# The expert stage of a graph and mixture-of-experts kernel in 68 pairs of 128-row halves, with the rows as weights of the first product

## The chip, the cores and the metric

The kernel runs on one core of one Trainium2 chip. The metric is the device time of one execution in microseconds; the number for a kernel is the median of its runs. The engines are named as the profile names them: PE is TensorE (PEld its weight loads), DVE is VectorE, ACT is ScalarE, POOL is GpSimd, and SP is SyncE, which issues most of the DMAs. A q behind a name (PEldq, SPq) is an engine's own queue: what waits, issues DMAs or computes register values there.

## The reference, cut to what matters

The input is 128 samples of 128 rows of 384 values, 16384 rows (tokens) in all. First come two graph layers per sample. Then each row goes through one of eight experts, the one that a small router gives the highest probability. Only this second half is touched.

```python
x = x + graph_layers(layernorm(x), adj, ...)          # (128, 128, 384)
# expert half: H = 384, R = 64, E = 8
def ffn(x, enc_w, enc_b, sw_w, sw_b, w1, b1, w2, b2):
    xt = x.reshape(-1, d)
    route_prob = softmax((xt @ enc_w + enc_b) @ sw_w + sw_b, axis=-1)
    route_prob_max, routes = max(route_prob), argmax(route_prob)
    onehot = one_hot(routes, E)
    h = einsum('td,edr->ter', xt, w1) + b1[None]
    h = gelu(h) * onehot[..., None]
    out = einsum('ter,erd->td', h, w2) + onehot @ b2
    return out * route_prob_max[:, None]
x = x + ffn(layernorm(x), ...)                        # layernorm: (x - mean) / sqrt(var + 1e-5)
```

## The kernel before

The program has two stages, each a block of five instruction streams, one for each engine, with semaphores between them; all engines meet at the border of the blocks.

**The graph stage** works on one sample at a time, two units of work a step in a software pipeline, and takes most of the time. Beside the graph layers it computes, for each finished sample, the layernorm's scale and shift and the router's choice, and scatters the rows into a DRAM buffer `buckets`, one region per expert, with an indirect DMA on GpSimd (L1236). A bucket row has 388 words: 384 values, the scale, the shift, the probability and the row's ID. After the last sample VectorE computes in `tile_table` (L1009 on) where each tile starts in `buckets` and which expert it has; eight expert numbers are packed in one word of `expert_words`.

**The expert stage** (L1358 on) cuts each expert's rows into tiles of 256 rows, T = 2 halves of P = 128. TILES is 16384 / 256 + 8 = 72, enough for every way in which the rows may fall on the experts; the last tile of an expert is moved back so that it ends with the expert's rows, and a row that comes twice gets an ID out of bounds (`again`), so that its second store is dropped. Everything is unrolled: `tiles` calls `step(i, i % 8)` on each engine for i from 0 to 76, and a step does several tiles at different points of the pipeline. For tile j:

- SyncE (`load`, L1415) reads the start row from `tile_row` and loads the tile into `tok`, a ring of eight, two neighbouring bucket rows (3104 bytes) to a partition. It does so only in the second block, after all scatters have landed.
- ScalarE and VectorE each normalise one half (L1492, L1541) into `n2_rows`; ScalarE also copies the expert's w1, doubled to 128 columns, into `w1_pick` (L1500), and its bias into `b1_pick` (L1504).
- TensorE turns the six 128 x 128 blocks (L1445, a turn is a product with the identity); ScalarE and VectorE copy them from PSUM to `n2T` (L1510, L1548).
- TensorE multiplies (`hidden`, L1457): weights `w1_pick` (128 columns), moving `n2T` (256 rows of the tile), three parts of the inner length 384. The type is f32, and each such product stands in the trace as two records. The result has the 64 hidden values twice, on 128 partitions, and the tile's rows along the columns.
- ScalarE applies GELU with the bias (L1519); VectorE splits the result into a high part and a low part (L1554, L1558), both on 128 partitions.
- TensorE multiplies each half with the expert's w2 (`output`, L1469 and L1470, type f32r, 384 columns, one record each), the address depending on the expert.
- VectorE combines product, probability and the row itself (`combine`, L1567); GpSimd adds `again` to the IDs (L1597) and stores each half with an indirect DMA (`store`, L1607).

TensorE's order in a step is turn(i-1), hidden(i-2), output(i-4); VectorE's is combine(i-5), normalise(i), copy_last(i-1), gelu_high(i-2), gelu_low(i-2). Each engine reads all nine expert words (`read_words`, L1398) before its first step.

## Time and profile before

| what | value |
|---|---|
| median of 3 runs | 2094.08 us (2093.04 to 2095.15) |
| the profiled execution, its own time | 2095.15 us |
| its span, first to last instruction | 2093.4 us |
| mean granted TensorE clock | 0.989 of full speed |
| graph stage, up to the border of the blocks | to about 1879 us |
| expert stage | about 1879 us to the end |
| first turn of the expert stage on TensorE | 1885.70 us |
| last store issued by GpSimd | 2089.22 us |
| TensorE busy over the span | 97% |

A span is what the instruction records cover; the time of a run has 1.75 us more here. TensorE runs at one of two clocks, 1.2 and 2.4 GHz; the profile shows what was granted as 0.50 or 1.00. The ends of matmuls are modelled, so the distance between the starts of two of them says more than a record's length. An idle time in brackets is that of the engine before the instruction, with what ended it; "issue" means that it waited for nothing that the profile shows. In the rows by stretch the five busy times are those of PE, PEld, DVE, ACT and POOL, in that order, and the last three numbers are the granted clock, the share of the time in which the 16 DMA engines were busy, and GB/s.

### The profile page before, as it was taken

To read this page: it belongs to the slowest core of one execution; us is meant where nothing else is said; L and a number is where in the kernel's file an instruction comes from. 1 tells how busy PE (TensorE), PEld (TensorE's weight loads), DVE (VectorE), ACT (ScalarE), POOL (GpSimd) and SP (SyncE) were. 2 spreads that over 40 slices of the span, in tenths; PEclk is the share of its full clock that TensorE was granted. 3 is DMA by queue.
4 is the path that set the end of the run, shared out by engine and by line. 5 is a ranking of instruction groups with operands and counts; after the bars stand their busy time and mean duration, and the time that the engine had idled before them with its cause. 6 is when DMAs were issued, how large, how long until landed. Compare 5 with 4: busy or idle time off the path is not lost. (4 is left out here: it accounts for less than half of the span.)

```text
span 2093.4 us, 48362 instructions
## 1 busy us (share of the span) xinstructions
PE 2029.2 (97%) x12059; PEld 1880.2 (90%) x12059; DVE 1689.7 (81%) x5206; ACT 1468.5 (70%) x3804; POOL 1403.7 (67%) x3342
## 2 busy tenths in 40 slices
PE   5999999999999999999999999999999999959997
PEld 4988899999999999999999999999999999948996
DVE  4788888888888888888888888888888888758997
ACT  4777777777677777777777776777777777627775
POOL 2556666666766666666666676666676666646887
PEclk9999999999999999999999999999999999979999
DMA  7011111221111111111111111111111111118895
GB/s 200 24 37 43 48 43 44 87 81 43 52 52 44 51 52 52 43 48 48 46 45 52 48 43 52 51 43 52 52 49 42 52 48 39 39 64 260 281 297 187
DMA packets 94358, 153.43 MB, mean 73 GB/s; under 512 B 17621, under 2 KB 70875, under 8 KB 94082
## 3 DMA queue, kind: packets, MB, share of 16 engines
q1 hardware_dynamic: 75972, 99.61, 16.4%
q0 software_dynamic: 17408, 50.62, 6.3%
q8 instruction: 103, 1.69, 0.3%
q14 instruction: 171, 1.40, 0.2%
q10 hardware_dynamic: 704, 0.10, 0.0%
HBM read 96.11 MB, written 57.32 MB: 73 GB/s over the span
## 5 line engine op out<-in xcount | busy, mean ns | idle before, releaser
L422 PE MATMUL bank<-wT_hi,own_hi 128*128 128x384 f32 x1536 | 513.6, 334 | 2.4 <-ACT bank L646 2.4
L424 PE MATMUL bank<-wT_hi,own_lo 128*128 128x384 f32 x1536 | 514.1, 335 | 0.0
L423 PE MATMUL bank<-wT_lo,own_hi 128*128 128x384 f32 x1536 | 513.2, 334 | 0.0
L436 PE MATMUL bank<-own_hi 128*128 128x512 f32 x768 | 324.0, 422 | 6.3 <-ACT bank L660 6.1
L438 PE MATMUL bank<-own_hi,own_lo 128*128 128x512 f32 x768 | 302.7, 394 | 0.0
L437 PE MATMUL bank<-own_lo,own_hi 128*128 128x512 f32 x768 | 300.2, 391 | 0.0
L422 PEld LDWEIGHTS bank<-wT_hi,own_hi 128*128 128x128 f32 x1536 | 288.4, 188 | 3.1 <-issue 1.9
L423 PEld LDWEIGHTS bank<-wT_lo,own_hi 128*128 128x128 f32 x1536 | 288.4, 188 | 0.0
L424 PEld LDWEIGHTS bank<-wT_hi,own_lo 128*128 128x128 f32 x1536 | 288.3, 188 | 0.0
L667 ACT ACTIVATE bank<-bank,sum_own 128x384 f32<-128x384 f32 x256 | 141.2, 552 | 206.7 <-issue 177.1
L1190 POOL TENSOR_TENSOR own_lo<-hT,own_hi 128x384 fp32r<-128x384 f32 x256 | 260.6, 1018 | 19.0 <-ACT own_hi L710 18.6
L1272 POOL TENSOR_TENSOR var_e<-mv,denom_sq 128x1 f32<-128x1 f32 x256 | 48.6, 190 | 235.7 <-DVE mv L858 235.6
L639 ACT ACTIVATE bank<-bank,neg_max 128x128 f32<-128x128 f32 x256 | 87.6, 342 | 164.6 <-DVE neg_max L826 164.6
L841 DVE CUSTOM_DVE_ANT_0 diagonal<-delta,ident 128x128 f32<-128x128 f32 x256 | 177.6, 694 | 9.0
L438 PEld LDWEIGHTS bank<-own_hi,own_lo 128*128 128x128 f32 x768 | 144.4, 188 | 33.3
L436 PEld LDWEIGHTS bank<-own_hi 128*128 128x128 f32 x768 | 145.1, 189 | 30.2 <-issue 7.2
L1607 POOL DMA_INDIRECT out_dram<-out_rows,row_ids x144 | 142.5, 989 | 43.9 <-issue 26.4
L1247 POOL TENSOR_SCALAR_AFFINE_SELECT deltaT_hi<-turned_hi 128x128 fp32r<-128x128 f32 x256 | 75.1, 293 | 141.7 <-ACT turned_hi L691 138.8
L660 ACT COPY bank<-own_seed 128x512 f32<-128x512 f32 x256 | 151.3, 591 | 22.5 <-ACT bank L667 0.4
L437 PEld LDWEIGHTS bank<-own_lo,own_hi 128*128 128x128 f32 x768 | 145.8, 190 | 22.9
L1236 POOL DMA_INDIRECT buckets<-rows,dest_words x128 | 138.8, 1084 | 29.4 <-issue 25.0
L863 DVE SCALAR_TENSOR_TENSOR bank<-bank,mv,gamma 128x384 f32<-128x384 f32 x256 | 157.9, 617 | 0.0
(213 smaller groups left out, 5590.1 us busy)
## 6 DMA issues: line engine op xcount, KB each, us to landing
tok<-buckets SPq DMA_DIRECT2D x72, 388.0 KB
x_in<-in_x_dram SPq DMA_DIRECT2D x128, 192.0 KB, 2.6
x_res<-in_x_dram SPq DMA_DIRECT2D x128, 192.0 KB
adj_in<-in_adj_dram SPq DMA_DIRECT2D x128, 64.0 KB, 2.6
buckets<-pads SPq DMA_DIRECT2D x9, 388.0 KB
out_dram<-out_rows,row_ids POOLq DMA_INDIRECT x144
buckets<-rows,dest_words POOLq DMA_INDIRECT x128, 2.8
w_top<-in_L_ffn_w_dram SPq DMA_DIRECT2D x2, 768.0 KB
```

Source lines behind the costliest of these rows:

```text
L422: pe.matmul(o, hi, w_hi(l, m, c), start=False, stop=False, skip_group_check=True)
L423: pe.matmul(o, hi, w_lo(l, m, c), start=False, stop=False, skip_group_check=True)
L424: last = pe.matmul(o, lo, w_hi(l, m, c), start=False, stop=(c == C - 1), skip_group_check=True)
L436: pe.matmul(own_bank[:], hi, own_w_hi, start=False, stop=False, skip_group_check=True)
L437: pe.matmul(own_bank[:], hi, own_w_lo, start=False, stop=False, skip_group_check=True)
L438: last = pe.matmul(own_bank[:], lo, own_w_hi, start=False, stop=(c == C - 1), skip_group_check=True)
L660: act.copy(own_bank[:], own_seed[:, u[1], WINDOW[k]]).then_inc(selfseed_ready, 1)
L667: act.activation(ctx_banks[odd][:, 0:D], own_bank[:, SELF[odd]], ACT.Copy, scale=sum_own[odd][:, 0:1]).then_inc(selfterm_ready, 1)
L841: dve.tensor_tensor_reduce(diagonal[:], delta[:], ident[:], 1.0, 0.0, ALU.mult, ALU.add, sum_own[odd][:]).then_inc(own_ready, 1)
L863: dve.scalar_tensor_tensor(o, o, mv[odd][:, 0:1], gamma[:, w[1], :], ALU.subtract, ALU.mult).then_inc(centred, 1)
L1190: pool.tensor_tensor(own_lo[:, l, :, SLOT[odd]], hT[:].rearrange("p (c t) -> p c t", c=C), own_hi[:, l, :, SLOT[odd]].bitcast(F32), ALU.su ...
L1607: pool.indirect_dma_start(out.rearrange("b s d -> (b s) d"), bass.IndirectOffsetOnAxis(ap=row_ids[k][:, t:t + 1].bitcast(U32), axis=0), ou ...
```

## The change

The expert stage works on halves of 128 rows, each with an expert of its own, two halves to a pair: 16384 / 128 + 8 = 136 halves, 68 pairs.

- **Loads.** Each half is loaded by itself, one row (1552 bytes) to a partition, into a ring of 24 halves. The first eight pairs' buffers lie where the graph stage held its incoming weights (`stage`), so the loads of the first pair are issued at the end of the first block, after the last scatter has landed; the others follow in the second block. A buffer is free when its half has been stored.
- **Layernorm.** Rows are no longer normalised. TensorE sums w1 over its 384 rows with a product of ones (`sum_w1`, three f32 products of 512 columns, behind the last graph product), VectorE takes the mean from w1 in place (`centre_w1`, three operations of 128 x 512), and the scale is applied after the product.
- **First product.** TensorE turns the raw rows; ScalarE copies a half's three blocks in one go (128 x 384). In `hidden` the turned rows are the weights and the expert's w1 (64 columns) moves, so the result has the rows on partitions. Its addresses depend on the expert, so w1 is not picked by ScalarE any more. VectorE scales and adds the bias (`scale`, two operations of 128 x 64), ScalarE applies GELU to the pair and doubles it, TensorE turns the result (two turns more), ScalarE casts the high part, VectorE subtracts the low part.
- **Second product** and combination are as before, with three PSUM banks instead of two for the results. The pair's IDs are adjusted by VectorE (`keep_ids`), in place; GpSimd only stores, in halves.
- **Expert words** (17 now) are read two a step, by TensorE and VectorE.
- The table computes two entries per partition, with four dependent steps more; `again` gets a function of its own. The constants b1 are loaded replicated on all partitions in one DMA.

TensorE's order in a step is turn of both halves of pair i, hidden(i-1), turn_gelu(i-2), output(i-3); VectorE's is combine(i-4), scale(i-1), keep_ids(i-1), gelu_low(i-2); ScalarE's is copy of both halves of i, gelu_high(i-2), gelu(i-1).

**TensorE in the steady part of the expert stage.** One tile of before, from its turns to the last product with w2:

```order
L1445 MATMUL bank<-ident,n_rows 128x128 x6
L1457 MATMUL bank<-n2T,w_pick 128x256 x3
L1469 REGISTER_ALU x2
L1469 ISA
L1469 MATMUL bank<-w_top,gelu_top 128x384
L1470 REGISTER_ALU
L1470 MATMUL bank<-w_bottom,gelu_bottom 128x384
L1469 MATMUL bank<-w_top,gelu_top 128x384
L1470 MATMUL bank<-w_bottom,gelu_bottom 128x384
```

Of one pair now, the turns and the start of the first half's products with w1 (`w_all` is w1; after it come two more products of this half, each with an address of its own, and then the second half likewise):

```order
L1484 MATMUL bank<-ident,stage 128x128 x6
L1495 REGISTER_ALU x2
L1495 ISA
L1495 MATMUL bank<-w_all,x1T 128x64
L1495 ISA
```

and what follows the second half's last product with w1, up to the first half's products with w2:

```order
L1495 ISA
L1495 MATMUL bank<-w_all,x1T 128x64
L1506 MATMUL bank<-ident,gelu_rows 128x128 x2
L1518 ISA
L1518 MATMUL bank<-w_top,gelu_top 128x384
L1519 REGISTER_ALU
L1519 MATMUL bank<-w_bottom,gelu_bottom 128x384
```

Six turns a pair stay; three products of 256 columns become six of 64 with an address each; two turns of `gelu_rows` are new; of the products with w2 each half now has its own address, since each half has its own expert.

**VectorE in the same part,** from one combination to the next, with what each instruction waits for. Before:

```order
L1541 TENSOR_SCALAR n_rows<-tok 128x384 [waits turned,tok_loaded3]
L1548 COPY n2T<-bank 128x256 [waits hidden_done,turned]
L1554 CAST gelu_top<-gelu_out 128x256 [waits y_done,gelu_ready]
L1558 TENSOR_TENSOR gelu_bottom<-gelu_out,gelu_top 64x256 [waits gelu_top_ready]
L1567 SCALAR_TENSOR_TENSOR out_rows<-bank,tok 128x384 [waits stored3,y_done]
L1567 SCALAR_TENSOR_TENSOR out_rows<-bank,tok 128x384 [waits y_done]
```

Now:

```order
L1581 SCALAR_TENSOR_TENSOR out_rows<-bank,tok 128x384 [waits stored0,y_done] x2
L1595 REGISTER_ALU [waits gelu_ready,hidden_done]
L1595 REGISTER_ALU
L1595 ISA
L1595 SCALAR_TENSOR_TENSOR before_gelu<-bank,tok,b_rep 128x64
L1595 REGISTER_ALU x2
L1595 ISA
L1595 SCALAR_TENSOR_TENSOR before_gelu<-bank,tok,b_rep 128x64
L1587 ISA tok<-tok,again 128x2x2
L1602 TENSOR_TENSOR gelu_bottom<-bank,gelu_top 64x256 [waits gelu_top_ready]
```

Three large operations (L1541, L1548, L1554) are gone from the row; two of 128 x 64 with register instructions ahead of them, behind the wait for the product, and the adjustment of the IDs stand there instead.

**SyncE at the border of the blocks.** Before, behind the last residual load:

```order
L336 UNCONDITIONAL_BRANCH
L1413 UNCONDITIONAL_BRANCH [waits barrier_Pool_Activation_PE_DVE_SP_release]
L1416 TENSOR_LOAD tile_row [waits scattered5,scattered6,scattered4,scattered7,scattered3,pads_stored,scattered2,tiles_ready,scattered1,scattered0]
L1416 ISA x2
L1421 ISA
L1421 DMA tok<-buckets 128x776
```

Now:

```order
L413 TENSOR_LOAD tile_row [waits scattered5,scattered6,scattered4,scattered7,scattered3,pads_stored,scattered2,tiles_ready,scattered1,scattered0]
L413 ISA x2
L414 ISA
L414 DMA stage<-buckets 128x388
```

The wait for the scatters and the first load, and a second one like it, moved ahead of the border.

The diff, cut to its core:

```diff
-    TILE = T * P
-    TILES = TOKENS // TILE + E
+    TILE = P
+    PAIRS = (TOKENS // TILE + E) // T
+    TILES = T * PAIRS
+    HELD, STAGED, AHEAD = 24, 8, 2
...
+                    for k in range(RING):
+                        sp.wait_ge(scattered[k], 16 * (B // RING))
+                    sp.wait_ge(pads_stored, 16 * (E + 1))
+                    sp.wait_ge(tiles_ready, 1)
+                    for h in range(AHEAD):
+                        row = sp.value_load(tile_row[0:1, h:h + 1], min_val=0, max_val=TAIL)
+                        sp.dma_start(early_tok[h // T][:, h % T, :], buckets[bass.ds(row, TILE), :]
+                                     ).then_inc(tok_loaded[h // T], 16)
...
+                    def sum_w1():
+                        pe.wait_ge(ffn_in, 16 * FFN_LOADS)
+                        pe.wait_ge(exp_done, UNITS)
+                        for c in range(C):
+                            last = pe.matmul(w1_sums_of, ones[:], w1_all[:, :, c, :], start=(c == 0), stop=(c == C - 1))
+                        last.then_inc(w1_summed, 1)
...
+                            if u and n == UNITS - 1:
+                                sum_w1()
...
+                    def centre_w1():
+                        dve.wait_ge(ffn_in, 16 * FFN_LOADS)
+                        dve.wait_ge(w1_summed, 1)
+                        for c in range(C):
+                            dve.scalar_tensor_tensor(w1_all[:, :, c, :], w1_sums_of, -1.0 / D, w1_all[:, :, c, :],
+                                                     ALU.mult, ALU.add).then_inc(w1_centred, 1)
...
                     def load(h):
                         row = sp.value_load(tile_row[0:1, h:h + 1], min_val=0, max_val=TAIL)
+                        if h >= HELD:
+                            sp.wait_ge(stored[(h - HELD) % OUTS // T], 16 * T * ((h - HELD) // OUTS) + 16 * T)
+                        sp.dma_start(tok[h % HELD // T][:, h % T, :], buckets[bass.ds(row, TILE), :]).then_inc(tok_loaded[h % HELD // T], 16)
...
-                            last = pe.matmul(o, w1_pick[k % 2][:, c, :, :].rearrange("p h r -> p (h r)"),
-                                             n2T[k % 2][:, c, :], start=(c == 0), stop=(c == C - 1))
...
+                    def hidden(s):
+                        pe.wait_ge(copied, T * s + T)
+                        if s >= 1:
+                            pe.wait_ge(scaled, T * s)
+                        for h in range(T * s, T * s + T):
+                            e = expert_in(words, h)
+                            for c in range(C):
+                                last = pe.matmul(hidden_of[:, h % T * R:(h % T + 1) * R],
+                                                 x1T[h % TURNED][:, c * P:(c + 1) * P], w1_all[:, e, c, :],
+                                                 start=(c == 0), stop=(c == C - 1))
+                        last.then_inc(hidden_done, 1)
+                    def turn_gelu(s):
+                        pe.wait_ge(gelu_ready, s + 1)
+                        if s >= 1:
+                            pe.wait_ge(gelu_top_ready, s)
+                            pe.wait_ge(gelu_bottom_ready, s)
+                        for t in range(T):
+                            last = pe.transpose(gelu_of[:, t * P:(t + 1) * P],
+                                                gelu_rows[s % PAIR_RING][:, t, :, :].rearrange("p d r -> p (d r)"), ident[:])
+                        last.then_inc(gelu_turned, 1)
...
+                    def scale(s):
+                        dve.wait_ge(hidden_done, s + 1)
+                        if s >= PAIR_RING:
+                            dve.wait_ge(gelu_ready, s - PAIR_RING + 1)
+                        for h in range(T * s, T * s + T):
+                            e = expert_in(words, h)
+                            dve.scalar_tensor_tensor(before_gelu[s % PAIR_RING][:, h % T, :],
+                                                     hidden_of[:, h % T * R:(h % T + 1) * R],
+                                                     tok[h % HELD // T][:, h % T, SCALE:SCALE + 1], b1_rep[:, e, :],
+                                                     ALU.mult, ALU.add).then_inc(scaled, 1)
...
+                    def step(i):
+                        if there(i):
                             for t in range(T):
+                                turn(T * i + t)
+                        if there(i - HIDDEN):
+                            hidden(i - HIDDEN)
+                        if there(i - TURN_GELU):
+                            turn_gelu(i - TURN_GELU)
                         if there(i - OUTPUT):
-                            output(i - OUTPUT, (k - OUTPUT) % RING)
+                            output(i - OUTPUT)
+                        read_words(pe, words, len(words), NEXT_WORDS)
...
+                    for h in range(TILES):
+                        store(h)
```

## Rows read from the trace of the kernel before

**Rows 1.** The page, part 1: busy us (share), instructions of each engine
```profile
PE 2029.2 (97%) x12059; PEld 1880.2 (90%) x12059; DVE 1689.7 (81%) x5206; ACT 1468.5 (70%) x3804; POOL 1403.7 (67%) x3342
```

**Rows 2.** By stretch: busy us (instructions) of five engines, granted clock, DMA
```profile
22.90:26.00 3.10, 2.78 (x18) 1.63 (x16) 2.71 (x7) 2.52 (x7) 0.00 (x0) 1.00 0.29 80
...
1886.00:1888.00 2.00, 2.00 (x11) 2.00 (x10) 1.23 (x3) 1.96 (x5) 0.61 (x2) 0.50 0.93 348
...
1900.00:1950.00 50.00, 50.00 (x302) 46.28 (x303) 46.81 (x114) 38.87 (x95) 40.88 (x57) 1.00 0.89 277
```

**Rows 3.** The chain that ended last, in the expert stage: start us, us
```profile
1962.60 1.30 PE bank L1457 x6
1963.89 0.17 PE bank L1469
...
1964.61 0.66 PE bank L1445 x6
1965.26 1.30 PE bank L1457 x6
```

**Rows 4.** Timeline of VectorE and GpSimd in one tile: start us, us, what
```profile
1961.94 0.99 POOL L1607 DMA_INDIRECT out_dram<-out_rows,row_ids  x1 [0.16 <-POOL row_ids L1597]
...
1962.10 0.42 DVE L1558 TENSOR_TENSOR gelu_bottom<-gelu_out,gelu_top 64x256 fp32r<-64x256 f32 x1
...
1962.45 1.12 DVE L1567 SCALAR_TENSOR_TENSOR out_rows<-bank,tok 128x384 f32<-128x384 f32 x2
...
1964.59 1.01 POOL L1607 DMA_INDIRECT out_dram<-out_rows,row_ids  x1 [0.16 <-POOL row_ids L1597]
```

**Rows 5.** Timeline, from TensorE's last turn to GpSimd's last store
```profile
2073.42 0.82 PE L1445 MATMUL bank<-ident,n_rows 128*128 128x128 f32 x6
...
2082.23 0.34 PE L1470 MATMUL bank<-w_bottom,gelu_bottom 128*128 x1
...
2087.94 0.97 POOL L1607 DMA_INDIRECT out_dram<-out_rows,row_ids  x1 [0.30 <-issue]
2089.22 0.97 POOL L1607 DMA_INDIRECT out_dram<-out_rows,row_ids  x1 [0.31 <-issue]
```

**Rows 6.** Timeline of TensorE: products with few moving columns, at either clock
```profile
915.28 0.31 PE L542 MATMUL bank<-one_hot,earlier 128*128 128x32 f32 x2
915.42 0.39 PE L543 MATMUL bank<-counts,ones 128*128 128x32 f32 x2
915.64 0.31 PE L455 MATMUL bank<-ident,delta 128*128 128x128 f32 x1
...
1868.66 1.43 PE L529 MATMUL bank<-one_hot,ones 128*128 128x24 f32 x6
1869.94 0.57 PE L533 MATMUL bank<-counts,ones 128*128 128x8 f32 x2
```

**Rows 7.** Line L1398, the value loads of expert words on TensorE's queue
```profile
L1398 PEldq TENSOR_LOAD <-expert_words x9: 295/307/494, 1879.5 to 1884.9; - x9
```

**Rows 8.** DMA queue 1, 500 to 1500 us and 1900 to 2070 us
```profile
q1 hardware_dynamic: 30663, 32.58, 10.9%
...
q1 hardware_dynamic: 9072, 25.03, 55.2%
```

**Rows 9.** Timeline, head of the expert stage
```profile
1880.73 8.46 SPq L1421 DMA_DIRECT2D tok<-buckets  x8
1880.75 2.93 DVE L1587 MEMSET gelu_bottom<- 1x256 f32 x8
...
1884.76 0.71 ACT L1492 ACTIVATE n_rows<-tok 128x384 f32<-128x384 f32 x1 [18.05 <-DMA tok<-buckets]
...
1885.70 2.79 PE L1445 MATMUL bank<-ident,n_rows 128*128 128x128 f32 x12 [8.31 <-ACT n_rows L1492]
```

**Rows 10.** Timeline, the last steps of the graph stage
```profile
1859.01 0.61 PE L542 MATMUL bank<-one_hot,earlier 128*128 128x32 f32 x2 [3.28 <-POOL counts L1228]
...
1865.34 0.19 DVE L930 TENSOR_TENSOR neg_logits<-bank,rows 128x32 f32<-128x32 f32 x1 [3.54 <-POOL rows L1200]
```

More of the change, by code:

```diff
@@ L1396, in read_words @@
[L1396 to L1410 removed]
+            OUTS, TURNED, Y_BANKS = 8, 4, 3
@@ new lines, in build, with pairs, read_words @@
+            hidden_of, gelu_of = bank[3][:, 0:T * R], bank[4][:, 0:T * P]
+            y_banks = (bank[5], bank[6], bank[7])
+            HIDDEN, TURN_GELU, OUTPUT, COMBINE = 1, 2, 3, 4
+            FIRST_WORDS, NEXT_WORDS = 1, 2
+            def pairs(eng, step):
+                for i in range(PAIRS + COMBINE):
+                    step(i)
+            def read_words(eng, words, first, count):
+                for b in range(first, min(first + count, TILES // RING)):
+                    words.append(eng.value_load(expert_words[0:1, b:b + 1], min_val=0, max_val=(1 << BITS * RING) - 1))
```

434 lines of the change are left out of this document (186 added, 248 removed).

## The prediction

> **What bounds the kernel now.** I read the totals of the engines first [rows 1]: TensorE is busy for 97% of the span, but that is one number over two stages, so it says only where to look next. The busy times by stretch [rows 2] separate them. The change leaves the loop of the graph layers alone; it works on the expert stage, which runs from about 1879 us to the end, some 214 us. In it TensorE is busy for all 50 us of a 50 us stretch, VectorE for 46.81, GpSimd for 40.88, ScalarE for 38.87, at a DMA share of 0.89. The chain of waits inside the stage [rows 3] is TensorE alone, step after step: 0.66 us for the six turns of a tile (L1445), 1.30 for the three f32 products with w1 (L1457, six records), and what is left to the next product, 2.66 - 1.96 = 0.70, for the four products with w2. So a tile of 256 rows costs 2.66 us of TensorE, 72 tiles 191.5 us, and nothing else is waited for.
>
> One resource stands right beside it. GpSimd issues two stores and adds the IDs once a tile: store to store of the same half is 2.65 us [rows 4]. When nothing holds it, at the end, its stores start 1.28 us apart, and the last starts 7.0 us after TensorE's last product [rows 5]. Its floor is therefore 2.56 a tile, with the IDs 2.66: freeing TensorE alone would have bought nothing.
>
> **The change, part by part.** *The number of tiles.* 72 tiles of 256 rows become 136 halves, 68 pairs. At today's 2.66 that would be 4 x 2.66 = 10.6 us less.
>
> *TensorE, one pair.* Turns of the raw rows: six, as now, 0.66. Two turns more, of GELU's rows: at 0.11 each (0.66 / 6), 0.22. Products with w2: four, as now, 0.70. The products with w1 are turned round: now w1 is the weights, 128 columns of it, and 256 columns move past them; then the turned rows are the weights and w1's 64 columns move. That is 6 products, 12 records, for 3 products, 6 records, and the moving columns fall from 6 x 256 to 12 x 64, to half. Were streaming the price, 12 x (1.30 / 6) x 64/256 = 0.65. But every record first loads 128 x 128 weights. The trace has f32 products with few moving columns [rows 6]: at the full clock, four records of 32 columns follow the turns in 0.36 us, 0.090 each, and the second pair of these takes 0.22, 0.11 each. At half the clock six records with 24 columns or less take 1.28, 0.213 each, twice 0.107, though they move almost nothing. So a record costs its weights. The bounds are 0.090 and 0.112; the long run of twelve is nearer to the steady second pair, with one quick record at its start: I take 0.109, 1.31 for the twelve. The halved streaming is paid back in full: 1.31 for 1.30. The pair costs 0.66 + 1.31 + 0.22 + 0.70 = 2.89 (bounds 2.66 and 2.92). 68 x 2.89 = 196.5 against 191.5: fewer rows, but 5 us more of TensorE.
>
> *Register instructions on TensorE's queue.* An address that depends on the expert now costs four a tile, then 14 a pair (two or so and three per half for w1, two per half for w2). The nearest rows are the value loads, three instructions of which one reads memory, every 0.67 us (1879.5 to 1884.9 for nine) [rows 7]: 0.22 each at most, next to nothing at least. 14 cost 0 to 3.1 us, beside 48 loads and products. They run ahead of the array while it works, so below about 2 us they cost nothing; I take 0.1 each, half of that bound, since these read no memory: 1.4, hidden. Reading the words of experts moves from the head of the stage into the first eight steps, two a step, 1.35 us a step on TensorE's queue, on top of 1.4: in about five steps this passes 2.89 a little. I take 1.5 us in all, bounds 0 and 5. VectorE does the same reads, partly under its 0.42 us subtraction [rows 4]: nothing.
>
> *The other engines.* VectorE loses the normalising of 128 x 384, a copy and a cast of 128 x 256 per tile and gains two 128 x 64 operations and an add of 128 x 4, each smaller than what goes; it keeps 1.12 for two combines and 0.42 for the low parts [rows 4]. From 46.81 / 50 x 2.66 = 2.49 it falls to about 2.1, and some 0.3 of register work after its wait for the product stands bare; 2.4 is under 2.89. ScalarE, at 38.87 / 50 x 2.66 = 2.07 now, gives its normalising, its pick of w1 and its pick of b1 for a second copy of 128 x 384 and a cast of 128 x 256: no more than 2.1. GpSimd is left with the stores, 2.56, under 2.89, so the queue of stores at the end goes. The stores' buffers are freed at the same depth (eight halves).
>
> *DMA.* A load is cut in two, with 1552 bytes per row instead of 3104 for two. In the first stage a MB of small packets on this queue costs 1000 x 16 x 0.109 / 32.58 = 54 us of engine time, in the expert stage 170 x 16 x 0.552 / 25.03 = 60 [rows 8]: small packets are not dearer. At 0.89 busy for 2.66 us now, the pair needs 2.4 of 2.89. Hidden; SyncE issues a load every 1.1 us (eight in 8.46 [rows 9]) against 1.45 us a half.
>
> *The head of the stage.* The two first loads are issued before the stages' border, behind the last scatter. That holds the border back by about 1.6 us, for SyncE needs 1.1 us a load. Then VectorE's fills, 2.93 us for eight single rows today [rows 9], are six and three larger ones, some 3.0 us; no normalising stands ahead of the first turn (now from 1884.76 to 1885.47). The stage opens at about 1881.1 (1879.5 today, four larger fills ahead of those at 1880.75, plus 1.6), and the first turn starts at 1881.1 + 3.0 + 0.4 = 1884.5, now 1885.70. Up to 1890 the clock is at its half level [rows 2]: step 0 takes 1.6, step 1 takes 6 x 0.213 + 12 x 0.213 = 3.9 (sum 1890.0), step 2 2.4 with a wait for the scaling, step 3 2.9: the fifth turn starts at 1895.4 (bounds 1893 and 1898).
>
> *The end.* 63 steps of 2.89 bring the last pair's turn to 1895.4 + 182.1 + 1.5 = 2079.0. From there: the step itself 2.9, 2.8 until VectorE begins to combine the last pair but two, 0.7 to its first store, then five stores at 1.28: 12.8, now 2089.22 - 2073.42 = 15.8 [rows 5]. The last store starts at 2091.8, 2.6 us later than now.
>
> *Ahead of the stage.* The sums of w1 (three f32 products, 512 columns) stand on TensorE behind the last graph product, where it now waits until the counts come at 1859.01 [rows 10]. At 2 x 512 columns per product they cost 3 x 2 x 2 x 0.217 = 2.6 us at full clock (0.217 is 1.30 / 6 for 256 columns), over by 1857.8; half of them at the half level, over by 1859.4 and up to 0.8 us late, with the turns behind them. The centring, three operations of 128 x 512 on VectorE, at the combine's rate 0.56 x 512/384 = 0.75 each, fits into the 3.54 us that VectorE idles before L930. The table has four dependent VectorE steps more, under 1 us, behind the last scatters. I take 0.4.
>
> **The sum.** 2.6 + 0.4 = 3.0 us on the profiled execution's 2095.15 us (span 2093.4, 1.75 outside): 2098.1. The median of the runs is 1.07 lower, so 2097.
>
> **What the Trainium skill would say.** The rows show that 24-column records are paced by their weights. The Trainium skill, "TensorE: Matmul & The Clock Gate", section "Architectural detail: the array is 16× 32×32, not 1× 128×128", states that a MATMUL can begin before its LDWEIGHTS completes; the quick record in rows 6 agrees for one record, and by it alone the twelve would cost streaming only, which is the first rival. The same page, "Part 4: PE-mode transpose", states that the fast clock doesn't engage for transposes; rows 2 have 18 turns (L568) and no other product between 22.90 and 26.00 us, at a granted clock of 1.00, so the trace disagrees, and what would follow is the third rival.
>
> **The rivals.** *1. Weights hide behind products.* Then the twelve cost 0.65 to 1.08 us and the pair 2.2 to 2.66 of TensorE; GpSimd's 2.56 to 2.6 or that 2.66 is the bound. 63 x (2.58 - 2.89) = -19.5, less some 2 us for stores queueing again at the end: 2080; at 0.090 a record, 2084. For it: the first pair in rows 6. Against it: the six records at the half level. Chance 0.15.
> *2. Slower: the queue is the bound.* If a register instruction costs 0.15 us rather than 0.1, 14 of them with waits and dispatch come to some 3.1 us in a row in which the array catches up with the queue; it decides from 2.89 on. 63 x 0.2 = +13: 2110. For it: three address instructions within 0.65 us of records per half, where there is none now. Chance 0.15. Its neighbour, the single bank for the products, which lets the next pair start only after VectorE has scaled: 1.3 + 1.0 + latencies = 2.5 today, with a late VectorE 3.05, 2107; chance 0.07.
> *3. The clock stays at or falls to 1.2 GHz,* since a pair has more turns and shorter products: everything on TensorE doubles to some 5.5 us, 68 x 2.6 = +177: 2274. Against it: turns alone held 1.00 [rows 2]. Chance 0.03.
> *That the change does less than it says,* rows no fewer, is excluded: 136 halves are fixed in the program.
>
> **How the numbers follow.** The main case, 0.60, spans 2093 to 2102 (start +-2, words 0 to 5, 2.87 to 2.92 a pair). This kernel's measurement can tell 0.2%, 4.2 us, from no change: 2089.9 to 2098.3. Of the main case 0.02 falls below, 0.34 within, 0.24 above. Faster: 0.15 + 0.02 = 0.17. Same 0.34. Slower: 0.24 + 0.15 + 0.07 + 0.03 = 0.49. The likeliest case's point, 2097, lies within. The range takes in the 0.090 price below and the queue above, 2083 to 2111, and leaves out about 0.07 below and 0.07 above.
>
> **What would show it.** In the new trace: L1495's records 0.11 us apart (0.06 would be rival 1); pairs 2.89 us apart; TensorE without idle time in the stage (gaps before L1495 or L1518 put down to issue would be rival 2); the stores 1.45 us apart in the steady part and idle time on GpSimd between them; the granted clock at 1.00 from about 1890; the first turn near 1884.5; the last store five or so us after the last product. Wrong from the root would be a steady bound that is not TensorE's: loads that land late, or VectorE without idle time.

## The result: 0.3% slower, and the profile after

The changed kernel took 2100.36 us (median of 8 runs, 2098.31 to 2104.30), the kernel before beside it 2094.98 (8 runs, 2093.04 to 2096.42): 1.0032 times the time before, 95% interval 1.0023 to 1.0040. Forecast were 2097 and a range of 2083 to 2111, with the larger chance on slower. The profiled execution took 2103.54 us, span 2101.8; it is one of the slower of the eight, which matters below.

The page, part 1, against [rows 1]: busy time, share of the span and instructions of each engine.

```profile
PE 2042.3 (97%) x12549; PEld 1902.6 (91%) x12549; DVE 1647.4 (78%) x5183; ACT 1432.0 (68%) x3716; POOL 1377.5 (66%) x3261
```

By stretch, against [rows 2]: busy time and instructions of the five engines, granted clock, DMA share, GB/s.

```profile
1883.20:1886.50 3.30, 2.60 (x12) 2.42 (x13) 0.53 (x2) 1.30 (x3) 0.00 (x0) 0.50 0.66 171
1886.50:1890.00 3.50, 3.50 (x19) 3.50 (x18) 0.50 (x3) 1.90 (x3) 0.00 (x0) 0.50 0.66 162
1890.00:1893.40 3.40, 3.38 (x17) 2.98 (x16) 0.13 (x2) 1.16 (x3) 0.00 (x0) 0.50 0.59 153
1893.40:1896.80 3.40, 3.40 (x18) 3.30 (x16) 0.98 (x4) 1.63 (x4) 0.00 (x0) 0.50 0.66 177
1896.80:1900.20 3.40, 3.40 (x16) 3.30 (x16) 1.47 (x5) 1.04 (x3) 0.00 (x0) 0.50 0.67 180
1900.20:1903.60 3.40, 3.40 (x31) 3.36 (x29) 1.62 (x6) 2.04 (x6) 1.99 (x2) 1.00 0.78 219
...
1950.00:2000.00 50.00, 49.93 (x415) 48.98 (x415) 34.40 (x104) 27.97 (x69) 34.13 (x35) 1.00 0.87 270
```

The last row is the steady stage. TensorE is busy for 49.93 of 50 us, as before, while VectorE fell from 46.81 to 34.40, ScalarE from 38.87 to 27.97 and GpSimd from 40.88 to 34.13: the change freed every engine but the one that sets the pace. The rows above it are the head: up to 1900.20 the granted clock stands at 0.50, the lower of the two levels, although TensorE is busy nearly all the time from 1886.5 on. In the kernel before, the upper level was back at 1890.

One pair in the steady part, the timeline of TensorE (start us, us, what), against [rows 3]:

```profile
1988.77 0.81 PE L1484 MATMUL bank<-ident,tok 128*128 128x128 f32 x6
1989.42 1.45 PE L1495 MATMUL bank<-w_all,x1T 128*128 x12
1990.71 0.39 PE L1506 MATMUL bank<-ident,gelu_rows 128*128 128x128 f32 x2
1990.85 0.42 PE L1518 MATMUL bank<-w_top,gelu_top 128*128 x1
1991.11 0.34 PE L1519 MATMUL bank<-w_bottom,gelu_bottom 128*128 x1
1991.29 0.34 PE L1518 MATMUL bank<-w_top,gelu_top 128*128 x1
1991.47 0.34 PE L1519 MATMUL bank<-w_bottom,gelu_bottom 128*128 x1
1991.64 0.81 PE L1484 MATMUL bank<-ident,tok 128*128 128x128 f32 x6
```

From start to start: turns 0.65, the twelve records with w1 1.29 (0.1075 each; 1.31 forecast), from GELU's turns to the next pair 0.93. The pair is 2.87 us; forecast were 2.89. The waits of GpSimd from 1905 to 2080 us (total, times, longest) show that the queue of stores is gone:

```profile
POOL out_dram L1633 <- DVE out_rows L1581: 39.6, 57, 2.3
```

The end of the program, from the last pair's turn to the last stores, against [rows 5]:

```profile
2084.24 0.82 PE L1484 MATMUL bank<-ident,stage 128*128 128x128 f32 x6
...
2090.37 1.12 DVE L1581 SCALAR_TENSOR_TENSOR out_rows<-bank,stage 128x384 f32<-128x384 f32 x2
...
2091.80 0.98 POOL L1633 DMA_INDIRECT out_dram<-out_rows,stage  x1 [0.57 <-DVE out_rows L1581]
...
2092.81 0.33 PE L1519 MATMUL bank<-w_bottom,gelu_bottom 128*128 x1
...
2098.25 0.98 POOL L1633 DMA_INDIRECT out_dram<-out_rows,stage  x1 [0.30 <-issue]
```

The last store starts 9.0 us later than before (2089.22), and 14.0 us after the last turn.

### The profile page after: what moved, and what is told of

It reads as the page before. It is cut to its first block and busy times, and to the rows that moved or that the text cites. A ratio compares the mean times of both kernels' runs of the same rounds, so it can differ in the third digit from the quotient of the medians.

```text
span 2101.8 us, 50079 instructions
## 1 busy us (share of the span) xinstructions
PE 2042.3 (97%) x12549; PEld 1902.6 (91%) x12549; DVE 1647.4 (78%) x5183; ACT 1432.0 (68%) x3716; POOL 1377.5 (66%) x3261
## 5 line engine op out<-in xcount | busy, mean ns | idle before, releaser
L689 ACT COPY bank<-own_seed 128x512 f32<-128x512 f32 x256 | 151.3, 591 | 22.4 <-ACT bank L696 0.4
L451 PEld LDWEIGHTS bank<-own_lo,own_hi 128*128 128x128 f32 x768 | 145.7, 190 | 22.4
L917 DVE TENSOR_TENSOR right_lo<-bank,right_hi 128x384 fp32r<-128x384 f32 x256 | 140.9, 550 | 18.3 <-ACT right_hi L714 17.2
```

Source lines behind the costliest of these rows:

```text
L451: pe.matmul(own_bank[:], hi, own_w_lo, start=False, stop=False, skip_group_check=True)
L689: act.copy(own_bank[:], own_seed[:, u[1], WINDOW[k]]).then_inc(selfseed_ready, 1)
L917: dve.tensor_tensor(right_lo[:], right_bank[:, 0:D], right_hi[:].bitcast(F32), ALU.subtract).then_inc(rightlo_ready, 1)
```

## The experiments

The theory: (a) the steady pair costs TensorE its number of records, each paced by its weights, so that halving the streamed columns bought nothing; (b) what came on top of the forecast is the late return of the clock at the head, and (c) the reads of expert words. The rivals: streaming counts after all, or something else than TensorE sets the pair (a); the clock follows nothing that the kernel does (b); the long early steps wait for rows (c).

The first four runs fell on a chip on which both kernels are slower (the kernel before 2158.49 us, 11 runs, mean granted clock 0.986; the changed one 2179.51, 0.978): in the traces of the changed kernel and its variants there, all engines stood still for some 3 us again and again in the expert stage, and the clock fell several times in it. Their times can be set beside each other only, with a spread of 5 to 12 us within a kernel; I use the head of the stage, ahead of the first such stretch. All other runs fell on chips like the first one. One more caution: the last product of the routing table (L658), ahead of everything that these edits touch, starts anywhere from 1875.5 to 1878.4 us in the profiles of the changed kernel and its variants, so places in the head are compared by their distance from it.

### More records: is TensorE the bound?

```
-                        for t in range(T):
+                        for t in (0, 1, 0, 1):
                             last = pe.transpose(gelu_of[...
```

> The two turns of GELU's rows are issued twice, so each pair has 50 TensorE records instead of 48; the result is the same. Theory (the steady pair is bound by TensorE's records and their weights, 0.107 to 0.112 us each): pairs 3.09 us apart instead of 2.87, 14.8 us more in all. Rival (the stores, the loads or a wait set the pair and TensorE has slack): 2.87 stays, no difference.

Measured: 2114.75 us (4 runs), 1.0094 (1.0077 to 1.0111) times before, 14.4 us over the changed kernel. TensorE in two successive pairs:

```profile
1981.70 0.82 PE L1484 MATMUL bank<-ident,stage 128*128 128x128 f32 x6
1982.35 1.45 PE L1495 MATMUL bank<-w_all,x1T 128*128 x12
1983.64 0.61 PE L1506 MATMUL bank<-ident,gelu_rows 128*128 128x128 f32 x4
...
1984.79 0.82 PE L1484 MATMUL bank<-ident,stage 128*128 128x128 f32 x6
```

The pair is 3.09 us: two turns more, 0.22 us more, in full on the time (68 x 0.22 = 15). Nothing else sets the steady part. By the same slope, the two turns of GELU's rows which the change itself added cost some 15 us over 68 pairs.

### Twice the columns: do they count?

```
-                                last = pe.matmul(hidden_of[:, h % T * R:(h % T + 1) * R],
-                                                 x1T[...], w1_all[:, e, c, :],
+                                first = min(c, C - 2)
+                                at = (1 + 3 * (h % T) + first - c) * R
+                                last = pe.matmul(hidden_of[:, at:at + 2 * R], x1T[...],
+                                                 w1_all[:, e, first:first + 2, :]...,
```

(Cut: VectorE reads its 64 columns from the new place in the result.)

> In all 68 pairs each product with w1 streams 128 columns instead of 64 (two of the expert's three blocks of w1, of which only the one wanted is read from the result), so the columns streamed are as many as in the kernel before. Theory (a record costs its weights, 0.107 to 0.112 us, and halving the columns bought nothing): pairs stay 2.87 us apart, time within 1 us of the unedited kernel. Rival (streaming counts, 0.65 us a pair): 3.5 us a pair, 44 us more.

Measured: 2100.99 us (5 runs, 2100.04 to 2103.50), 1.0032 (1.0020 to 1.0045). In the steady part:

```profile
1981.51 0.82 PE L1484 MATMUL bank<-ident,tok 128*128 128x128 f32 x6
1982.16 1.50 PE L1497 MATMUL bank<-w_all,x1T 128*128 x12
1983.51 0.38 PE L1508 MATMUL bank<-ident,gelu_rows 128*128 128x128 f32 x2
...
1984.43 0.82 PE L1484 MATMUL bank<-ident,tok 128*128 128x128 f32 x6
```

Twelve records of 128 columns take 1.35 us, of 64 columns 1.29; the pair 2.92 instead of 2.87. Doubling the columns costs 0.05 us where the rival said 0.65. The time is 2.1 us above the unedited kernel beside it (2098.90), not within 1 us as expected; 68 x 0.05 = 3.4 us would account for it. So up to 128 columns an f32 record costs nearly the same whatever it streams. That the weight load is this price is the likely reading, as each record has one; a fixed price per record of another kind would look the same, and no run here changes the size of the weights. Above 128 columns streaming does count. In one of the four runs on the slower chip the first three pairs streamed 192 columns (more on it below); the twelve records of its first pair read as in the first fence, and with 64 columns on the same chip as in the second:

```profile
1888.49 3.46 PE L1499 MATMUL bank<-w_all,x1T 128*128 x12
```
```profile
1886.14 2.66 PE L1495 MATMUL bank<-w_all,x1T 128*128 x12
```

From start to the next turn's start that is 3.30 us against 2.46, although the clock rose at 1891.2, so that the last 0.6 us of the 3.30 ran at the upper level already. The second pair, all at the upper level, needs 2.05 us for its twelve records (1893.26 to 1895.31), 0.17 each against 0.1075.

The Trainium skill, "TensorE: Matmul & The Clock Gate", section "Architectural detail: the array is 16× 32×32, not 1× 128×128", lets a MATMUL begin before its LDWEIGHTS is complete. Whatever of that holds for a single record, a row of them got no cheaper by it here: 1.29 us at 64 columns, 1.35 at 128.

### The clock: the same kernel again

> The changed kernel unedited, once more, on a chip shared with the three runs beside it (the first such run fell on the slower chip). Expected 2100.4 us, 1.0026 times the kernel before. For the clock: the profile of the changed kernel had it back at 1900.2, three other profiles of it or its near variants at 1895.5 to 1896.6, so here 1896; the first four steps after it 3.4 to 3.7 us long.

Measured: 2098.90 us (6 runs, 2098.39 to 2103.92), 1.0027 (1.0015 to 1.0038) times the kernel before beside it (2095.23). The expected time was 1.5 us off, the expected clock wrong: in its profiled execution (2098.76 us) the upper level was back at 1886.1, ten microseconds earlier than expected.

```profile
1882.80:1886.10 3.30, 3.15 (x15) 2.97 (x16) 0.10 (x1) 1.69 (x4) 0.00 (x0) 0.51 0.65 170
1886.10:1890.00 3.90, 3.45 (x30) 3.11 (x30) 0.64 (x3) 2.68 (x5) 0.00 (x0) 1.00 0.70 162
```

And its turns of the first pairs, with those of the first profile of the changed kernel (second fence):

```profile
1882.95 2.86 PE L1484 MATMUL bank<-ident,stage 128*128 128x128 f32 x12 [6.31 <-DVE gelu_bottom L1621]
...
1890.97 0.85 PE L1484 MATMUL bank<-ident,stage 128*128 128x128 f32 x6 [0.62 <-issue]
...
1894.54 0.85 PE L1484 MATMUL bank<-ident,stage 128*128 128x128 f32 x6 [0.50 <-issue]
```
```profile
1883.90 2.87 PE L1484 MATMUL bank<-ident,stage 128*128 128x128 f32 x12 [6.31 <-DVE gelu_bottom L1621]
...
1893.56 1.49 PE L1484 MATMUL bank<-ident,stage 128*128 128x128 f32 x6
...
1899.07 1.37 PE L1484 MATMUL bank<-ident,stage 128*128 128x128 f32 x6
```

The fifth turn follows the first after 11.59 us here, after 15.17 there; the ninth after 25.99 (1908.94) and 29.53 (1913.43). So the same program has more than one way through its head, here 3.5 us apart. A third stands in its profile on the slower chip (below): clock back at 1895.5, the fifth turn 13.77 us after the first. Of the 14 runs of the changed kernel on such chips, seven have a mean clock of 0.991 or more over the whole program: 2098.31 to 2100.11, median 2098.76. Seven have less: 2099.65 to 2104.30, median 2102.98. The mean clock is a rough sorter only, as it counts every fall: between 29 and 51 us, too, the clock falls once in both of these profiles, not at all in some others and twice in others. The kernel before has a spread of its own: of the 19 runs beside this one, four lie at 2092.3 to 2093.3, with a mean clock of 0.990, and fifteen at 2094.9 to 2096.6, with 0.987 to 0.989. Its range is 4.3 us here (4.8 in another 19 runs), that of the changed kernel's eight first runs 6.0, so the edit at most widened a spread that was there.

What is different in the two profiles: in both TensorE first does twelve turns at the lower level. In one the rise comes 3.2 us after the first of them. In the other it does not come with the turns, and then not while 64-column products fill the engine either (36 of them from 1886.55 to 1897.4, busy 13.68 of the 13.7 us up to 1900.2 in the rows above); it comes after the first products with w2 (384 columns, from 1897.65). Those wide products are not what it takes, though. In each of the other five profiles with a late rise (1895.5 to 1896.8) the clock rose among the 64-column products of the third pair, before the first product with w2; in the one on the slower chip, the products came first:

```profile
1894.42 1.99 PE L1495 MATMUL bank<-w_all,x1T 128*128 x12
1896.39 0.42 PE L1518 MATMUL bank<-w_top,gelu_top 128*128 x1
```

The kernel before has 256-column products behind its first turns and has the clock back 4.3 us after the first of them. Three runs speak for the columns as a cause. With 128 columns all five runs had a mean clock of 0.991 or more, and the profiled one its rise at 1885.6. With 192 columns in the first three pairs, on the slower chip, the rise came at 1891.2, 5.4 us after the first turn, against 12.0 us in the unedited kernel there, as had been expected; the time had been expected to fall by 1 to 2.5 us and did not (2182.26 us against 2179.51, within that chip's spread), for the wider records cost more and the fifth turn came no earlier (13.94 us after the first, 13.77 unedited). And the filled head, of which two such products behind the routing table are cut here:

```
+                    for _ in range(2):
+                        pe.matmul(bank[7][:, 0:D]..., ident[:], w1_all[:, 0:D // R, 0, :], start=True, stop=True)
```

> Four f32 products of 384 columns are added where TensorE is idle: two behind the last product of the routing table, two at the head of the expert stage ahead of the first turn; their results are never read. Theory (the clock came back late because turns and 64-column products at the lower clock don't bring it back, wide ones do): the granted clock rises by 1890 or before instead of at 1900, steps 1 to 3 take 3.5 us each instead of 3.8, 4.6 and 5.5, and the time falls by 2 to 3 us to 2098. Rival (the clock follows something else than TensorE's own work, or a fixed time after it fell): rise at 1900 as before, 2100.4 or up to 0.5 us more.

Measured, on the slower chip: 2179.37 us against 2179.51. The granted clock did what the theory says; by stretch, the filled kernel, and the unedited one (second fence) on that chip:

```profile
1884.70:1886.30 1.60, 1.60 (x9) 1.57 (x8) 0.00 (x0) 0.53 (x2) 0.00 (x0) 0.50 0.62 152
1886.30:1890.00 3.70, 2.91 (x24) 2.57 (x22) 0.64 (x3) 3.01 (x6) 0.00 (x0) 1.00 0.63 172
```
```profile
1893.00:1895.40 2.40, 2.40 (x14) 2.39 (x12) 0.98 (x4) 1.63 (x4) 0.00 (x0) 0.50 0.68 179
1895.60:1900.00 4.40, 4.40 (x37) 4.18 (x36) 2.41 (x8) 2.01 (x5) 0.14 (x1) 1.00 0.66 181
```

The upper level is back at 1886.3 instead of 1895.5. Counted from the table's last product (1876.76 here, 1876.08 unedited), the first turn comes 7.97 us after it instead of 7.40, so the fill holds it back by 0.6 us, and the fifth 19.19 instead of 21.17 (1895.95, 1897.25): a gain of 2.0 us at the fifth turn, at the lower edge of the expected 2 to 3, which the median of the times does not show on this chip. That columns are the cause is likely, not shown: six profiles of the changed kernel or near relatives had the late rise (11.6 to 16.3 us after the first turn), and the four with more columns at the head an earlier one (1885.6 to 1887.3, and 1891.2), but the unedited kernel had an early one too. A rival is open: the executions also differ in how long after the clock's fall the first turn comes, 20.8 us in the unedited profile with the early rise and 20.9 in that with 128 columns, 21.2 to 22.5 in the six late ones. The filled one (22.3) and the one with 192 columns (21.9) speak against this as the only cause; no run here varies it alone.

The unedited run and the one on the reads, on the same slower chip:

> The changed kernel once more, unedited, as the point of comparison on this chip. Expected: 2100.4 us, 1.0026 times the kernel before (0.2 to 0.4% slower), pairs 2.87 us apart, granted clock back at its upper level only some 9 to 10 us after 1890, the first four steps after it 3.4 to 3.7 us long instead of 2.87.

Measured: 2179.51 us (6 runs), 1.0091 (1.0069 to 1.0114) times the kernel before; clock back at 1895.5, the steps behind it 3.54 and 3.64 us. Pairs are 2.87 us apart only between the standstills.

> One word of experts is read per step instead of two (seventeen steps instead of eight), nothing else. Theory (TensorE's queue is what made steps 4 to 7 last 3.43 to 3.70 us: 1.35 us of reads on top of the address instructions): a single read fits under 2.87 us, steps 4 to 7 fall to 2.87 to 3.0, the time falls by 2.5 to 2.9 us to about 2097.6. Rival (these steps wait for rows that land late, or for VectorE): they stay at 3.4 to 3.7, 2100.4.

Measured: 2179.48 us (6 runs), no difference; the first two steps in question are 2.88 and 3.05 us there instead of 3.54 and 3.64, but the standstills bury it.

To see whether a filled head is worth anything to the kernel before, products of the same kind were put there, two of 256 columns behind the routing table and four of 384 at the head of the stage, and that kernel was profiled once more on a chip like the first:

> Control for the filled head: the same kind of f32 products added to the kernel before, two of 256 columns behind the routing table and four of 384 at the head of the stage. If the late clock is of the change, this gains little: the clock was back at 1890 anyhow, rise now by 1886.6, steps 1 and 2 3.44 and 2.02 us become 3.2 and 2.0, the first turn up to 0.5 us later: within 1 us of the kernel before. If the fill is worth as much here as in the changed kernel (2 to 3 us), the clock explains none of the difference between the two.

Measured: 2099.34 us (10 runs), 1.0020 (1.0010 to 1.0029): 4 us slower, where within 1 us was expected. The first turn is held back from 1885.7 to 1888.57, for here the fill came behind the nine value loads, which already use up the time. The clock was back at 1888.2. As a control it is poor: it shows that the fill buys nothing in this kernel, and no more.

> The kernel before, unedited, for its profile on the same chip as the runs beside it. On the chip of the four runs just made both kernels were slower (2158 and 2180 us), and the changed one showed stretches of some 3 us in which all engines stood still, every 17 to 27 us of the expert stage, each followed by a reading of the lower clock. If this comes from the chip, the kernel before shows the same number of such stretches there; if the change brings it, it shows none. On a chip like the first one: 2095 us, tiles 2.66 us apart without a break.

Measured: 2096.56 us, tiles 2.65 to 2.66 us apart but for two steps of 3.6 and 3.3, clock back at 1890.1, as in the first profile of it. It fell on a chip like the first one, so it doesn't say whether this kernel stands still on the other; its 2158.49 us there say that most of that loss isn't the change's.

### The reads of expert words

```
-            FIRST_WORDS, NEXT_WORDS = 1, 2
+            FIRST_WORDS, NEXT_WORDS = 1, 1
```

> One word per step instead of two, again, where nothing else disturbs the steps. Theory (the reads hold TensorE's queue up): steps 4 to 8 last 2.9 to 3.1 us instead of 3.4 to 3.7, the time falls by 2 to 2.9 us against the unedited kernel beside it, to some 2098. Rival (reads of the first steps are only spread, and their sum comes back at 0.1 to 0.2 us in each of seventeen steps): 1 us or less.

Measured: 2100.64 us (12 runs, 2096.62 to 2104.16), 1.0025 (1.0016 to 1.0033). Two words a step, in the unedited kernel at the upper clock level, and one word a step (second fence):

```profile
1904.44 0.34 PE L1519 MATMUL bank<-w_bottom,gelu_bottom 128*128 x1
1905.37 0.85 PE L1484 MATMUL bank<-ident,stage 128*128 128x128 f32 x6 [0.59 <-issue]
```
```profile
1904.03 0.33 PE L1519 MATMUL bank<-w_bottom,gelu_bottom 128*128 x1
1904.48 0.84 PE L1484 MATMUL bank<-ident,stage 128*128 128x128 f32 x6
```

With two, TensorE reaches the next turn 0.93 us after its last product starts (0.17 without reads), put down to issue: its own queue is busy reading. With one it is 0.45. The steps fall to 2.87 to 3.45 us, the first half of the theory. The second doesn't hold: seventeen steps now have a read. From the fifth turn to the eighteenth, thirteen steps at 2.87 would be 37.3 us; the unedited kernel needs 40.3, this one 40.4. For these steps the rival holds: the reads were spread, and their sum came back. The median is 1.7 us above the unedited kernel beside it (2098.90), but seven of the twelve runs here are below a mean clock of 0.991 and two of the six there. Sorted by it, there is a gain of 2 us only where the first steps are likely to run at the upper level; at the lower one a step of 3.8 to 5.5 us would hide its reads anyhow, which is argued, as only a run of the late kind was profiled. The five runs with a mean clock of 0.991 or more are 2096.62 to 2099.05, median 2096.75, against 2098.39 to 2099.04, median 2098.7, of the four such runs of the unedited kernel beside it; the runs with less lie in the same place for both (2100.17 to 2104.16, and 2102.48 and 2103.92). So late clock and reads seem to hide each other. The next run removes both.

> The filled head and one word per step together, on the changed kernel. If the late clock and the reads are the two terms that I had too small, the eighth turn after the first comes some 23 us after it instead of 29.5 (1883.90 to 1913.43), the time is 5 to 6 us under the changed kernel and within 1 us of the kernel before: 2095. If the two hide each other in part: 2097 to 2098.

Measured: 2098.95 us (10 runs, 2096.31 to 2100.50), 1.0020 (1.0010 to 1.0029); nine of the ten at a clock of 0.991 or more. The ninth turn comes 22.4 us after the first (1885.20 to 1907.55), as expected; yet the time is only 1.4 us under the changed kernel's median, not 5, and above the expected 2097 to 2098 of the second case, too. The fill costs 0.5 us ahead of the first turn (7.88 us after the table's last product, unedited 7.43), eight more steps have a read in them (27.6 us for the next nine, unedited 25.9), and the expectation compared with the profile that had the latest clock. No version made here beats the kernel before.

### The two early loads

```
-    HELD, STAGED, AHEAD = 24, 8, 2
+    HELD, STAGED, AHEAD = 24, 8, 0
```

> The two first loads of rows are issued behind the stages' border, as all others. By my sum the border then comes 1.6 us to 2 us earlier (1880.3 in the changed kernel, 1878.4 here), the fills with it, and the first turn waits for the rows instead: issued from 1879.3 and 1880.4, landing 2.6 to 3.6 us later, first turn 1883.0 to 1884.0 against 1883.90, time within 0.5 us. If the early loads were worth their place, the first turn would come after 1884.9 and the time rise by 1 us.

Measured: 2102.71 us (4 runs, 2102.17 to 2103.65), 1.0038 (1.0023 to 1.0052), 3.8 us above the unedited kernel beside it, where 0.5 was expected. The head of the stage, and in the second fence that of the changed kernel:

```profile
1876.77 1.12 PE L658 MATMUL bank<-ident,per_tile_twice_wide 68*128 68x68 f32 x4 [1.49 <-DVE per_tile_twice_wide L1107]
...
1879.25 0.82 DVE L1617 MEMSET gelu_bottom<- 64x256 f32 x3 [0.96 <-PEq L344]
...
1883.80 1.51 PE L1484 MATMUL bank<-ident,stage 128*128 128x128 f32 x6 [5.91 <-DMA stage<-buckets]
1886.04 0.47 PE L1484 MATMUL bank<-ident,stage 128*128 128x128 f32 x1 [0.73 <-DMA stage<-buckets]
```
```profile
1876.47 1.12 PE L658 MATMUL bank<-ident,per_tile_twice_wide 68*128 68x68 f32 x4 [1.49 <-DVE per_tile_twice_wide L1107]
...
1880.74 0.82 DVE L1617 MEMSET gelu_bottom<- 64x256 f32 x3 [2.75 <-PEq L344]
```

Counted from the table's last product (L658), the fills begin 2.48 us later without the early loads and 4.27 with them: the border was held back by 1.8 us, forecast 1.6. The first turn comes 7.03 us after that product instead of 7.43, now waiting for rows, but the next pair's turn 9.27 instead of 8.76 (1885.23). The early loads are worth 0.5 us at the second pair. All four runs are of the late clock, median 2102.7 beside 2103.0 for the seven such runs of the unedited kernel: no difference in the time where the clock is alike. That they were all late may come of the gap in the first turns, or of chance; this wasn't tested.

## Why the prediction was right, step by step

The mechanism held, and the median lies in the range, but 3.3 us above the point of the sum: a loss of 2 to 3 us was summed up, 5.4 were measured. The upper bound of the range was set by the rival of TensorE's queue, which did not come; that it also covered a clock that no term allowed for was luck.

The sum was made for the profiled scale (2098.1), the profiled execution took 2103.54. The difference of 5.4 us, by the prediction's own steps:

- **The pair.** Forecast 2.89 us, measured 2.87; its central argument, that a record has a price below which fewer columns buy nothing and that halving the columns is paid back in full, held (1.31 forecast for the twelve records, 1.29 measured), and the two experiments with more records and more columns show it. The value of 0.109 for a record came from the few-column products in [rows 6]. The first rival, weights hidden behind products, is excluded: it wanted records 0.06 us apart, they are 0.1075.
- **The other engines and the DMA.** All under the pair: VectorE 34.40 / 50 x 2.87 = 1.97 us a pair (forecast 2.4), ScalarE 1.61, DMA 0.87 busy at 270 GB/s. Neither the queue nor the single bank for the products became the bound in the steady part, the second rival; single steps of 3.0 to 3.2 us, the two longest at the same pairs in both unedited profiles, add 1.4 us, which no step of mine had; their cause is open.
- **The head.** The first turn came at 1883.90, forecast 1884.5, and at 1882.95 in the repeated profile, a difference that lies ahead of the stage. The price of the held-back border was right (1.6 forecast, 1.8 measured).
- **The clock.** Forecast: back at 1890, the fifth turn at 1895.4. Measured 1900.2 and 1899.07 in this execution, 1886.1 and 1894.54 in the other. This step was mis-sized, and more than that it had one answer where there are several. I had taken the clock's return from the row of the kernel before without asking what had brought it back there: 256-column products, which the change takes away. It is +4.3 us here, counted from the first turn; 3.5 of the 4.8 us between the two profiled executions lie there and 1.0 ahead of the stage. The turns alone were read too favourably, too: the row with a granted clock of 1.00 in [rows 2] shows turns that kept a level which stood there before them; it doesn't show them bringing it back, and after them the clock fell, at 29.8 us.
- **The reads of the words.** Forecast 1.5 us (0 to 5), measured 2.9 from the fifth to the ninth turn alone (14.36 us for four steps, 11.5 at 2.87). Reads did not hide under the array's work as I had put it: a step with two reads is 0.7 us too long, also where the upper level had been back for long (14.40 us for these four steps in the repeated profile).
- **The 63 steps** from the fifth turn to the last: 185.2 us, forecast 183.6. The smaller pair gives back 1.3, the reads take 1.4 more, the stray steps 1.4.
- **The end.** 14.0 us, forecast 12.8. VectorE begins to combine the last pair but two 6.1 us after the last turn (5.7 forecast), and the first of the last six stores 1.4 us after it (0.7 forecast): GpSimd was at another store until 2091.23 and then idle for 0.57 us, put down to VectorE's rows; then five at 1.29, as in [rows 5].
- **Ahead of the stage.** Forecast +0.4; nothing of it is seen, though the spread of 2.9 us there would cover it. The centring lies in VectorE's idle time, as forecast. The sums of w1 kept the clock at 1.00 until 1862.65 (1855.89 before):

```profile
1854.74 2.74 PE L495 MATMUL bank<-w_all,ones 128*128 128x512 f32 x6
...
1861.01 1.89 DVE L1121 SCALAR_TENSOR_TENSOR w_all<-bank,w_all 128x512 f32<-128x512 f32 x3
```

In sum: -0.6 (first turn) + 4.3 (clock) + 1.6 (steps) + 1.2 (end) = 6.5 us at the last store, less 0.4 taken for the part ahead of the stage, which is in the first turn, less 0.6 for a shorter tail behind the last store (5.3 us, before 5.9): 5.5 of 5.4. The repeated profile with the early clock took 2098.76 us on the same scale, 0.7 from the 2098.1 of the sum, with its fifth turn at 1894.54 and its last at 2079.39 (forecast 1895.4 and 2079.0). That is so near by luck in part: the first turn was 1.6 us early, and the clock was back 3.9 us before the forecast 1890, while the steps from the first turn to the fifth took 0.7 more than forecast, the 63 steps 1.3 and the end 1.3. The medians of the two sets of runs, 2100.36 and 2098.90, lie between those of the two groups. The third rival, a clock at the lower level for the whole stage, did not come; a piece of it did, from 1890 to 1900.2.

## What to carry to other kernels

Count the records that an f32 product gives TensorE before its columns: here, from 128 moving columns down to 64, streaming fewer gained 0.05 us in twelve records, and turning the product round on half-sized tiles doubled the records. An edit that frees three engines and leaves the bound one 0.2 us longer per step is a loss, however much idle time appears elsewhere: 68 steps of 2.87 us are more than 72 of 2.66. And where a stage begins at the lower clock, look at what brought the clock back before: if the change takes that work away, give the return two values and carry both into the sum.

## What the runs showed of the hardware

- Twelve f32 records with 128 x 128 weights at the upper clock level: 1.29 us at 64 moving columns, 1.35 at 128, 2.05 at 192; at the lower level some 0.21 us each at 64 (2.46 us for twelve).
- The upper clock level came back 3.2 us after a row of turns began in one execution. In another of the same program it did not while TensorE was fully busy for 13.7 us, the first 11 of them with 64-column products and turns alone, and in five more profiles it came back some 12 us after the first turn, among 64-column products. The Trainium skill, "TensorE: Matmul & The Clock Gate", "Part 4: PE-mode transpose", says that the fast clock doesn't engage for transposes; the execution with the early rise had twelve turns and three records of products ahead of it (1882.80 to 1886.10), so it did engage with next to nothing else. The late rises neither agree nor disagree, since 64-column products, of which the sentence says nothing, stood among the turns.
- A value load a step on TensorE's queue lengthened steps of 2.87 us by 0 to 0.6 us, 0.24 on average over thirteen; two in a step by 0.7.
- On one of the chips the kernel before took 63 us more and the changed one 79. The traces of the changed one show standstills of all engines there, and no cause of them; the kernel before wasn't profiled there.
